# A third bank for the attention scores, and one bank less for the stages around them

## The chip, the cores and the metric

The kernel runs on 1 core of one Trainium2 chip. The metric is the device time of one execution in microseconds. The kernel before took 2009.88 us in the median of 3 runs (2007.78 to 2009.91).

## The reference

The input x has 8 sequences of 1024 tokens with 256 features, all in float32. Three blocks follow one another, each added to x:

```python
x = x + 0.5 * ffn(layernorm(x))      # before attention
x = x + attn(layernorm(x))
x = x + 0.5 * ffn(layernorm(x))      # after attention

def ffn(x):                          # same weights both times
    logits = x @ R.T                                 # 8 experts
    gate = softmax(logits) * (one of the top 2)      # then gate / (sum + 1e-6)
    h = einsum('btd,erd->bter', x, A)                # rank 16 per expert
    return x @ W.T + b + einsum('bter,eor->bto', gate[..., None] * h, B)

def attn(x):
    kv = rmsnorm(x @ W_kv) * g_kv                    # rank 64
    q_c = x @ W_q                                    # rank 128
    k = concat(heads(kv @ W_kdec, 16), rope(heads(x @ W_krope, 32)))
    q = concat(heads(q_c @ W_qdec, 16), rope(heads(q_c @ W_qrope, 32)))
    v = heads(kv @ W_vdec, 16)                       # 16 heads
    scores = q @ k.T / sqrt(48), causal
    return softmax(scores) @ v, heads joined, @ W_o
```

## The kernel before, in words

**Tiling.** A sequence is cut in two halves of 512 tokens. The feed-forward parts and the projections work on one half at a time: a "job" (16 jobs before attention, 16 after). Attention works on "quads": 4 heads of one sequence, 32 quads in all, g = 0 to 31. Lane 0 runs 30 jobs one after the other. Lane 1 runs two alone, job 1 at the start and the last one, job 31; its tiles are carved out of `probs`, so in the trace its tiles read `probs`.

**A job on PE.** Each step of a job fills one PSUM bank, which ACT or DVE then empties: tr0, tr1 (transposes of the normed rows, two token tiles each, L692), low0, low1 (low-rank part and gate logits, L699), gated_tr (L704), y0, y1 (main product, L712 and L714); before attention also tr20, tr21 (L692), qc (L721), kv (L727) and kvt (L733); after attention wo0 and wo1 come first (L681). `wj_b` has 2 banks for lane 0, and the steps take them in turn: step number `use` waits until step `use - 2` has been emptied (L666 to L672). Lane 1 takes `o_b` and the second bank of `st_b` in turn. ACT empties most steps (L951); DVE empties wo (L1038) and y (L1132) by adding them to `xa`.

**A quad on PE.** "mx" steps multiply q by k without a mask (48 a quad, L787, 2 banks `mx_b`); DVE takes the row maximum of each (L977, L980). The maxima are folded, transposed ("mx_turn", L793) and sent through a scratch tensor in HBM into the row `SHIFT` of the q tile, so that the score matmul subtracts them. "score" steps compute the transposed scores: 12 strips of 4 heads, each step two matmuls, L755 and L757, into one bank of `st_b`. ACT takes the exponential of each into `probs` (L859), GpSimd zeroes the masked corner (L1169), and "pv" steps (6 a quad, L775) multiply by v into `o_b`. DVE divides (L1002 to L1015), SyncE writes the result to `ao_scratch`, and the job after attention reads it back.

`st_b` has 2 banks. Score number i writes bank `a % 2`, a being the head, and waits for exponential i - 2 (L750). Score matmuls and mx matmuls use float32r; the others use float32. "piece" and "v" steps (L821 to L834) make k, q and v from the projections in the one bank `tp_b`; ACT, GpSimd and DVE apply rope and split each into a high and a low part, and SyncE sends them through HBM scratch into the tiles of the quads.

**The order.** There is no scheduler at run time. A table `ORDER` has one string for each engine, and each letter takes the next step of one stream: on PE, S is a score, X an mx step, V a pv, P a piece, table or v, F an mx_turn, J a step of lane 0 and j one of lane 1. Each engine walks its string in order (`walk`); semaphores alone hold the engines together. Each string is 3892 steps on PE, 2107 on ACT, 2741 on DVE, 543 on GpSimd and 528 on SyncE.

PSUM has 8 banks here: st_b 2, mx_b 2, o_b 1, tp_b 1, wj_b 2.

Of the kernel before, what the change touches and what calls it, by code (L numbers as in the profile page):

```python
# [130 lines left out]
def uses(*steps):  # L131

    out = []
    for n, (m, pair, side) in enumerate(UNIT):
# [1109 lines left out]
```

## Time and profile before

| what | value |
|---|---|
| median of 3 runs | 2009.88 us |
| profiled execution | 2005.28 us |
| its span | 2002.8 us |
| PE busy | 1901.2 us, 95% |
| DVE busy | 1439.5 us, 72% |
| ACT busy | 1024.3 us, 51% |
| GpSimd busy | 849.4 us, 42% |
| mean granted TensorE clock | 0.98 |

All durations come from the profiled execution; the span is that of its instructions, and the execution took 2.5 us more. PE is the matmul row of TensorE and PEld its weight loads, which overlap it. Idle before a row is the idle time of that engine just before it, and the arrow names what ended it. One float32 matmul stands as two rows in the trace and as one in the order.

### The profile page before, as it was taken

Reading aid. Unit: us, or ns where it says so; the run is one execution under the profiler, and the core shown is the slowest. Engines: PE = TensorE matmul, PEld = TensorE weight load, DVE = VectorE, ACT = ScalarE, POOL = GpSimd, SP = SyncE. Lnnn points to the kernel's source line nnn. Section 1 sums busy time; section 2 is a strip of 40 time slices with the busy share of each in tenths; the row PEclk is TensorE's granted clock in tenths of the full one; section 3 lists DMA queues with packets and bytes.
Section 4 is the critical chain, followed back from the end, with each engine's and each line's share of the span. In section 5 each row is a group of like instructions: output and inputs, shape, how many; then the busy total and the mean of one; then the engine's idle time right before and its main releaser. Section 6 shows DMA issues by size and latency. Waiting matters only on the chain.

```text
span 2002.8 us, 32215 instructions
## 1 busy us (share of the span) xinstructions
PE 1901.2 (95%) x10832; PEld 1325.5 (66%) x10832; DVE 1439.5 (72%) x4555; ACT 1024.3 (51%) x2125; POOL 849.4 (42%) x912
## 2 busy tenths in 40 slices
PE   6789999999999999999999999999999999999995
PEld 5446766666677666766677667666767667677554
DVE  5767777777776877778777777788777687677632
ACT  3436554555454554545555545555556455454450
POOL 3446453553433635255441644435453454422121
PEclk9979999999999999999999999999999999999997
DMA  3687666676665666676566576646677566665511
GB/s 101 191 207 173 169 153 173 163 173 152 174 157 123 175 159 162 164 168 162 152 155 162 145 196 161 167 115 171 168 166 196 129 172 160 159 155 122 116 33 45
DMA packets 169812, 307.58 MB, mean 154 GB/s; under 512 B 15088, under 2 KB 33776, under 8 KB 169648
## 3 DMA queue, kind: packets, MB, share of 16 engines
q1 hardware_dynamic: 169648, 305.53, 61.0%
q8 instruction: 86, 1.41, 0.3%
q14 instruction: 78, 0.64, 0.1%
HBM read 179.12 MB, written 126.35 MB: 153 GB/s over the span
## 4 chain that ended last, share of the span: by engine, by line
PE 68%; DMA 10%; DVE 8%; POOL 7%; ACT 2%; issue 2%; SPq 1%; POOLq 0%; DVEq 0%; ACTq 0%
PE st_b L755 12%; PE o_b L775 11%; PE mx_b L787 11%; PE st_b L757 10%; PE tp_b L824 4%; PE wj_b L712 4%; DMA st<-k_scratch 3%; PE tp_b L821 3%; PE wj_b L681 2%; PE wj_b L714 2%; DMA q_scratch<-lo_t 2%; PE wj_b L699 2%; DVE xn L1077 2%; PE wj_b L692 2%; DVE mx_b L977 1%
## 5 line engine op out<-in xcount | busy, mean ns | idle before, releaser
L859 ACT ACTIVATE probs<-st_b 128x512 f32<-128x512 f32 (+3 forms) x1536 | 708.3, 489 | 537.9 <-PE st_b L757 504.4
L977 DVE CUSTOM_DVE_ANT_0 mx_b<-mx_b,tri 128x256 f32<-128x256 f32 (+3 forms) x1024 | 511.0, 515 | 141.2 <-PE mx_b L787 136.9
L755 PE MATMUL st_b<-st 97*128 97x512 f32 (+2 forms) x1536 | 588.2, 387 | 10.6 <-ACT probs L859 6.8
L787 PE MATMUL mx_b<-st 96*128 96x256 f32 (+2 forms) x1536 | 565.5, 411 | 12.4 <-DVE mx_s L980 6.3
L757 PE MATMUL st_b<-st,k_st 96*128 96x512 f32 (+2 forms) x1536 | 533.4, 351 | 0.0
L1169 POOL TENSOR_SCALAR_AFFINE_SELECT probs<-probs 128x512 f32<-128x512 f32 x256 | 168.2, 660 | 607.9 <-ACT probs L859 607.5
L980 DVE TENSOR_REDUCE mx_s<-mx_b 128x1 f32<-128x512 f32 (+1 forms) x512 | 333.2, 651 | 117.0 <-PE mx_b L787 110.4
L787 PEld LDWEIGHTS mx_b<-st 96*128 96x128 f32 x1536 | 282.0, 191 | 169.6 <-issue 80.1
L755 PEld LDWEIGHTS st_b<-st 97*128 97x128 f32 x1536 | 293.1, 191 | 134.7 <-issue 61.4
L757 PEld LDWEIGHTS st_b<-st,k_st 96*128 96x128 f32 x1536 | 294.9, 192 | 33.0 <-issue 9.8
L775 PE MATMUL o_b<-probs,v_s 128*17 128x512 f32 (+3 forms) x3072 | 285.7, 490 | 2.0 <-POOL probs L1169 1.9
L775 PEld LDWEIGHTS o_b<-probs,v_s 128*17 128x17 f32 x3072 | 70.9, 97 | 142.8 <-issue 111.7
L977 DVE DVE_READ_ACCUMULATOR2_ANT mx_s<- 128x1 f32 x1024 | 143.2, 140 | 0.0
L523 POOL TENSOR_TENSOR rot<-rot,cos_t 128x512 f32<-128x512 f32 x62 | 79.1, 1276 | 148.6 <-ACT rot L872 148.5
L872 ACT ACTIVATE rot<-tp_b 128x512 f32<-128x512 f32 x124 | 74.0, 597 | 107.1 <-PE tp_b L824 65.5
L712 PE MATMUL wj_b<-w_s,xt 128*128 128x256 f32 x480 | 123.9, 380 | 1.3 <-ACT xn L951 1.3
L907 ACT ACTIVATE hi_t<-rot 128x1024 fp32r<-128x1024 f32 x62 | 65.6, 1058 | 104.3 <-POOL rot L529 104.1
L824 PE MATMUL tp_b<-stg,wkr_s 128*128 128x512 f32 x240 | 114.9, 601 | 1.6 <-ACT rot L872 0.9
L1132 DVE SCALAR_TENSOR_TENSOR xa<-wj_b,xa 128x512 f32<-128x512 f32 x60 | 41.4, 690 | 89.3 <-PE wj_b L714 89.2
L1192 POOL TENSOR_TENSOR xa<-xa,hb_s 128x256 f32<-128x256 f32 x120 | 93.1, 802 | 24.8 <-DVE xn L1077 24.8
L1077 DVE TENSOR_SCALAR xn<-xa,mv,rs 128x256 f32<-128x256 f32 x180 | 95.4, 577 | 7.0 <-POOL rs L1185 5.8
L712 PEld LDWEIGHTS wj_b<-w_s,xt 128*128 128x128 f32 x480 | 88.6, 190 | 13.2 <-ACT xn L951 2.4
(189 smaller groups left out, 2302.7 us busy)
## 6 DMA issues: line engine op xcount, KB each, us to landing
st<-q_scratch SPq DMA_DIRECT2D x128, 384.0 KB, 5.9
st<-k_scratch SPq DMA_DIRECT2D x128, 384.0 KB, 8.7
k_st<-k_scratch SPq DMA_DIRECT2D x128, 384.0 KB, 10.4
q_scratch<-hi_t SPq DMA_DIRECT2D x32, 768.0 KB, 3.8
q_scratch<-lo_t SPq DMA_DIRECT2D x32, 768.0 KB, 5.2
k_scratch<-hi_t SPq DMA_DIRECT2D x30, 768.0 KB, 4.3
k_scratch<-lo_t SPq DMA_DIRECT2D x30, 768.0 KB, 4.6
ao_scratch<-o_f SPq DMA_DIRECT2D x256, 32.0 KB, 1.8
```

The lines of the kernel that those rows point to most:

```text
L712: nc.tensor.matmul(dst, xt[:, tk, P * kk:P * kk + P], w1_s[:, kk, 0:D], start=(kk == 0), stop=False)
L755: nc.tensor.matmul(dst, k1_st[u][0:SHIFT + 1, a, P * j:P * j + P], q_st[u][0:SHIFT + 1, a, q0:q0 + w], start=True, stop=False)
L757: nc.tensor.matmul(dst, k2_st[0:SHIFT, a, P * j:P * j + P], q_st[u][0:SHIFT, a, q0:q0 + w], start=False, stop=True).then_inc(st_full, 1)
L775: last = nc.tensor.matmul(o_b[32 * a:32 * a + DV + 1, 0, q0 - HALF * h2:q0 - HALF * h2 + n], v_s[g // NQ % 2][:, j, HQ * q + a, :], probs[ ...
L787: nc.tensor.matmul(mx_b[:, m % 2, 0:w], q_st[u][0:SHIFT, a, P * i:P * i + P], k1_st[u][0:SHIFT, a, k0:k0 + w], start=True, stop=True).then ...
L824: last = nc.tensor.matmul(dst, wkr_s[:, kk, k, eight], own.stg[:, :, P * kk:P * kk + P], start=(kk == 0), stop=(kk == KD - 1))
L859: nc.scalar.activation(probs[:, a, PLACE[s]:PLACE[s] + n], st_b[:, a % 2, HALF - n:HALF], ACT.Exp, scale=SCALE).then_inc(exp_done, 1)
L977: nc.vector.tensor_tensor_reduce(src, src, tri[:, HALF - n:HALF], 1.0, NEG, ALU.add, ALU.max, dst).then_inc(mx_done, 1)
L980: nc.vector.tensor_reduce(dst, src, AX_X, ALU.max).then_inc(mx_done, 1)
L1077: last = nc.vector.tensor_scalar(own.xn[:, tk, :], own.xa[:, tk, :], own.mv[:, tk, 0:1], own.rs[:, tk:tk + 1], ALU.subtract, ALU.mult)
L1169: nc.gpsimd.affine_select(out=d, in_=d, compare_op=ALU.is_ge, fill=0.0, base=0, pattern=[[0, HQ], [1, P]], channel_multiplier=-1).then_inc ...
L1192: last = nc.gpsimd.tensor_tensor(own.xa[:, k, :], own.xa[:, k, :], hb_s[:, :], ALU.add)
```

## The change

`st_b` gets 3 banks and `wj_b` keeps 1. Score i takes bank `i % 3` and waits for exponential i - 3. Each lane has one bank (`wj_b` for lane 0, `o_b` for lane 1), so every step of a job waits until the step before it has been emptied. Lane 1 no longer uses `st_b`, so the first scores no longer wait for job 1. All five strings of `ORDER` are replaced; they hold the same number of each letter as before.

```diff
@@ ORDER, one line of 38 of the PE string @@
-        "SXSXSXVXXPSXSXPXSXSPXXSSXXXXXFXXPXXVSSXPXXSSPXXSSXSXSXJFXXSSXVXXSSXJXXSSXPXSXSPXXSSPXXSSVXXSSJXSXSPXXSSV"
+        "SSXPXSXSSPXXSSSVXXXXXXPXXVPXXFXXPXXXXJXXJXXSSXSXSJXXSSSXXFSSXSXSXSSXSXSSXSXSSSXXVXXPSXXSSPXSXSSXSPXXSSSVX"
...
-        st_b = bank("st_b", 2)
+        st_b = bank("st_b", 3)
         mx_b = bank("mx_b", 2)
         o_b = bank("o_b")
         tp_b = bank("tp_b")
-        wj_b = bank("wj_b", 2)
-        lanes = [Lane(sb, [wj_b[:, 0, :], wj_b[:, 1, :]], sb("stg", [P, GT, STGW]), sb("kvs", [P, GT, P]), ""),
-                 Lane(carve, [o_b[:, 0, :], st_b[:, 1, :]], probs[:, :, late:late + STGW],
+        wj_b = bank("wj_b")
+        lanes = [Lane(sb, [wj_b[:, 0, :]], sb("stg", [P, GT, STGW]), sb("kvs", [P, GT, P]), ""),
+                 Lane(carve, [o_b[:, 0, :]], probs[:, :, late:late + STGW],
...
-            return lanes[LANE[n]].banks[bank_use(n, name) % 2]
+            return lanes[LANE[n]].banks[0]
...
-                if name == "wo0" and use:
+                if use:
                     pe.wait_ge(own.wj_free, use)
-                elif use > 1:
-                    pe.wait_ge(own.wj_free, use - 1)
...
                         pe.wait_ge(row_set, g + 1)
-                        pe.wait_ge(lanes[1].wj_free, len(job_mm(1)))
-                    if i > 1:
-                        pe.wait_ge(exp_done, i - 1)
+                    if i > 2:
+                        pe.wait_ge(exp_done, i - 2)
                     w = max(n, WIDE)
-                    dst = st_b[:, a % 2, HALF - w:HALF]
+                    dst = st_b[:, i % 3, HALF - w:HALF]
...
-                    nc.scalar.activation(probs[:, a, PLACE[s]:PLACE[s] + n], st_b[:, a % 2, HALF - n:HALF], ACT.Exp,
+                    nc.scalar.activation(probs[:, a, PLACE[s]:PLACE[s] + n], st_b[:, (UNITS * g + HQ * s + a) % 3, HALF - n:HALF], ACT.Exp,
```

Three places of the order follow. The line numbers of the changed kernel are smaller: L749 and L751 are the score (before L755 and L757), L781 is mx, L690 a transpose, L697 low, L702 gated_tr, L708 and L710 y, L679 wo, L769 pv.

PE, a middle quad, around the steps low0 and low1 of a job, before:

```order
L787 MATMUL mx_b<-st 128x512
L699 MATMUL wj_b<-w_s,xt 128x136 x4
L787 MATMUL mx_b<-st 128x512
L755 MATMUL st_b<-st 128x384
L757 MATMUL st_b<-st,k_st 128x384
L787 MATMUL mx_b<-st 128x512
L755 MATMUL st_b<-st 128x384
L757 MATMUL st_b<-st,k_st 128x384
L699 MATMUL wj_b<-w_s,xt 128x136 x4
```

and the corresponding place after:

```order
L749 MATMUL st_b<-st 128x256
L751 MATMUL st_b<-st,k_st 128x256
L749 MATMUL st_b<-st 128x256
L751 MATMUL st_b<-st,k_st 128x256
L781 MATMUL mx_b<-st 128x384
L697 MATMUL wj_b<-w_s,xt 128x136 x4
L781 MATMUL mx_b<-st 128x512
L781 MATMUL mx_b<-st 128x384
L697 MATMUL wj_b<-w_s,xt 128x136 x4
```

Before, a score stood alone between mx steps and several steps lay between low0 and low1; after, scores come in pairs or threes, and two mx steps lie between low0 and low1.

PE, the end of the last quad, before (the last gated_tr, a score, y0 and y1, pv, then wo0 and wo1 of lane 1 in two banks):

```order
L704 MATMUL wj_b<-ident,xn 128x128 x4
L755 MATMUL st_b<-st 128x256
L757 MATMUL st_b<-st,k_st 128x256
L712 MATMUL wj_b<-w_s,xt 128x256 x2
L714 MATMUL wj_b<-bt_s,xn 128x256
...
L775 MATMUL o_b<-probs,v_s 17x256 x4
L775 MATMUL o_b<-probs,v_s 17x128 x4
L681 MATMUL o_b<-wo_s,probs 128x256 x4
L681 MATMUL st_b<-wo_s,probs 128x256 x4
```

and after:

```order
L749 MATMUL st_b<-st 128x256
L751 MATMUL st_b<-st,k_st 128x256
L769 MATMUL o_b<-probs,v_s 17x256 x4
L769 MATMUL o_b<-probs,v_s 17x128 x4
L702 MATMUL wj_b<-ident,xn 128x128 x4
L708 MATMUL wj_b<-w_s,xt 128x256 x2
L710 MATMUL wj_b<-bt_s,xn 128x256
...
L679 MATMUL o_b<-wo_s,probs 128x256 x8
```

The last pv has moved ahead of gated_tr, y0 and y1 of lane 0, and lane 1's wo0 and wo1 share one bank.

SyncE, the head, around the first shift (L643 sends it, L647 reloads it as a row, L613 stores a unit of q or k, L624 loads a half of a quad), before:

```order
L624 DMA st<-q_scratch 48x4x512 x2
L624 DMA st<-k_scratch 48x4x512 x2
L643 DMA shift_scratch<-shift 16x128
L624 DMA st<-q_scratch 48x4x512 x2
L624 DMA st<-k_scratch 48x4x512 x2
L647 DMA st<-shift_scratch 1x4x512
L613 DMA q_scratch<-hi_t 384x1x512
L613 DMA q_scratch<-lo_t 384x1x512
```

and after:

```order
L613 DMA q_scratch<-hi_t 384x1x512
L643 DMA shift_scratch<-shift 16x128
L613 DMA q_scratch<-lo_t 384x1x512
L647 DMA st<-shift_scratch 1x4x512
L624 DMA st<-q_scratch 48x4x512 x2
L624 DMA st<-k_scratch 48x4x512 x2
```

The four loads between shift and row have moved behind the row, and the two stores have moved ahead of them.

## Rows read from the trace of the kernel before

**Rows 1.** The page, busy time of each engine and share of the span.

```profile
PE 1901.2 (95%) x10832; PEld 1325.5 (66%) x10832; DVE 1439.5 (72%) x4555; ACT 1024.3 (51%) x2125; POOL 849.4 (42%) x912
```

**Rows 2.** Timeline of a middle quad: start us, us, engine, line, operation, tiles, shapes.

```profile
1023.00 0.40 PE L755 MATMUL st_b<-st 97*128 97x512 f32 x1
1023.23 0.40 PE L757 MATMUL st_b<-st,k_st 96*128 96x512 f32 x1
```

**Rows 3.** Windows: us, busy of PE, PEld, DVE, ACT, POOL, clock, DMA, GB/s.

```profile
0.00:50.00 50.00, 33.84 (x164) 27.83 (x165) 29.59 (x120) 19.30 (x32) 19.41 (x32) 0.93 0.33 102
...
1000.00:1100.00 100.00, 99.59 (x584) 72.02 (x581) 74.54 (x243) 53.76 (x111) 32.47 (x37) 1.00 0.66 158
...
1950.00:2003.00 53.00, 27.22 (x119) 22.08 (x118) 12.13 (x45) 4.46 (x12) 6.62 (x10) 0.77 0.13 42
```

**Rows 4.** Waits of the weight loads, whole span: us in total, times, longest.

```profile
PEld st_b L755 <- issue: 61.4, 138, 1.9
PEld st_b L755 <- ACT probs L859: 45.7, 146, 1.1
...
PEld mx_b L787 <- DVE mx_s L977: 30.9, 98, 2.3
PEld mx_b L787 <- DVE mx_s L980: 26.9, 65, 2.5
...
PEld wj_b L712 <- ACT xn L951: 2.4, 3, 1.0
```

**Rows 5.** Timeline of the last quads: one score kept back.

```profile
1907.11 0.28 PE L755 MATMUL st_b<-st 97*128 97x256 f32 x1
...
1907.23 0.28 PE L757 MATMUL st_b<-st,k_st 96*128 96x256 f32 x1
...
1907.75 0.19 PEld L755 LDWEIGHTS st_b<-st 97*128 97x128 f32 x1 [0.44 <-ACT probs L859]
1907.75 0.39 PE L755 MATMUL st_b<-st 97*128 97x256 f32 x1 [0.23 <-ACT probs L859]
...
1907.97 0.28 PE L757 MATMUL st_b<-st,k_st 96*128 96x256 f32 x1
```

**Rows 6.** Groups by shape, ACT and DVE: busy us, mean ns, idle before.

```profile
L859 ACT ACTIVATE probs<-st_b 128x512 f32<-128x512 f32 x768 | 436.5, 595 | 273.7 <-PE st_b L757 253.1 <-PE o_b L775 8.6
...
L1132 DVE SCALAR_TENSOR_TENSOR xa<-wj_b,xa 128x512 f32<-128x512 f32 x60 | 41.4, 690 | 89.3 <-PE wj_b L714 89.2
```

**Rows 7.** Timeline of the head: a bank filled, emptied, and the next matmul.

```profile
26.93 0.60 PE L704 MATMUL wj_b<-ident,xn 128*128 128x128 f32 x4
...
27.57 0.60 ACT L951 ACTIVATE xn<-wj_b 128x512 f32<-128x512 f32 x1
...
28.31 1.10 PE L712 MATMUL wj_b<-w_s,xt 128*128 128x256 f32 x4 [0.78 <-ACT xn L951]
```

**Rows 8.** Timeline of the end.

```profile
1952.21 1.10 PE L712 MATMUL wj_b<-w_s,xt 128*128 128x256 f32 x4 [0.54 <-ACT xn L951]
1952.30 0.63 POOL L1169 TENSOR_SCALAR_AFFINE_SELECT probs<-probs 128x512 f32<-128x512 f32 x1 [1.40 <-ACT probs L859]
...
1957.56 0.84 PE L775 MATMUL o_b<-probs,v_s 128*17 128x256 f32 x16
...
1967.98 3.64 PE L681 MATMUL o_b<-wo_s,probs 128*128 128x256 f32 x8 [9.58 <-DMA probs<-ao_scratch]
...
1980.70 2.18 PE L699 MATMUL o_b<-w_s,probs 128*128 128x136 f32 x8
```

**Rows 9.** Waits of the weight loads from 1900 us on.

```profile
PEld st_b L755 <- ACT probs L859: 9.3, 26, 0.7
```

**Rows 10.** Timeline of the head: weights landed, the shift row, the first score.

```profile
15.41 0.69 DVE L1069 COPY lo_t<-sin_s 128x1024 f32<-128x1024 f32 x1 [3.10 <-DMA sin_s<-in_sin]
...
113.74 0.73 SPq L647 DMA_DIRECT2D st<-shift_scratch  x1
...
121.00 0.80 PE L755 MATMUL st_b<-st 97*128 97x512 f32 x1 [0.47 <-DMA st<-shift_scratch]
```

More of the change, by code:

```diff
@@ new lines @@
+        "XSSSJXSXSXSXSVXXSSSXSXSSPXXSSSPXXSSSFXXJPXXJVXXJPXXSSXSXSSXSXJXSSSXSXSXFVXXPXSXSXSXSXPXXVPXXSSSXSXPXJXVX"
+        "XJXXSSSJXXSSSPXXSSSPXXSSSPXXSSSSXJXVFXXJSXXSSXSXJXXSSSJXXSVXXVSXXSSSJXSSXSSXSXSSXSFXSSXSXSVXXPXSXSSSXPXV"
+        "JXXSPXXSSSXXVXXPXXSSSXVXXSSSXPXXSSSPXXSSSVXXSSSXSXFSXSXSXSXSPXXSSSVXXSSSPXXSSSSXXSSSXSXSSPSSSFVPSSXXSPXX"
+        "SVXXJPXXSSSXSXJXXVXXPXXSSPXXSSSXSXSJXXSSSVXXSSSXVXXSSSXXSSSXVXXSSSXSSXSFXSSVXXJSXSXJXXSSJXXSSSXSXSSXSXSS"
+        "SXSXSSXXFVXSXSXSSJXXVXXJSVXXJXXSSJXXSSSPXXSSSPXXSJSXSSXJXXSSJXXSSSXSPXSXSSVXXSSSPSSSJSXPJXXVFJXXPJXXVXXS"
@@ new lines @@
+        "SSXSXSSXPXSSSXSSXJXSSJXXSSJFXXVXXPXSSXXSSPXXVXXPSXXSSPXXSSSVXXSJSXSSXJXSSXSJXXSSXJXSSXSSXSSXPXXSSSPXXVFX"
+        "XJPXXSSJXXSSSVXXSJXXSSSXSXSSXSXSSSXVXFXVSXSXSSJXSXSJXSXSJXXVXXJXXSSSXPXSXSXSPXJXSPXXJXXSSSJXXSSSPXXSSSXV"
+        "XXPXSXSSJSXXFSJXSXPJXXSSVJXXSSSXPXSSSPXSSXSSXSXSPXVPJSSSJFSVJXXPSXSXSXSPXXVXPXXSSSXSXPXVXXVXXSSXSXSXSSSS"
+        "XSSXSVXXSSJSXSXJXSSXXJSXSXJXSXSSVFXXSSSXSXSSVXXSSSSXXSSXSXSSXXJSXSXJXXSSJFXXSSSXVXXSSXSXSVXXVXXJSSSXJXSS"
+        "XJXXSSSJXXSSSPXXSSSXSXSJXSXSJXXSSJXXSSSPXXSVXPXSXSSXVFXXSSVXXPXXSSSPJXXSSJXXSSJXXSJXXSSSXSXPSXSXSVXXSFSS"
@@ new lines @@
+        "XPJXSXPJXXPJXXPVXXPSXXSSSXSXSSPXXSSSVXXSSSPXXSSJSXSXJXSSXJXSXJXSXFSXSVXXPXSXSSVXXSSSSSXSXSSXSXJSXSXJXXSS"
+        "JFXXSVXXVSXXSSSXXSSSVXXJSSXJXSXSJXXSSJXXSPXSXSSPXXSSJXPXJXXSSSJXXSSPXXVVXXSSSXPSJSXFXSSJXXPJXXSSSJXXSSSX"
+        "SSXSPXSSXPXSXSPVXPJSSFSJPSJPVXXPXXSSXSXSXPXXVXXSVXXSSXSXVXXSSSXSXSSXSXSSXSVXXSSSJXXJXXJXSXJXSXSXSSVFXXSS"
+        "SXSXSSXSXSVXXSSSXSXSSXSXJXSSXJXXSSJFXXSSSXSXSSXSXVXXSVXXSSJXSXSJXSXSJXXSSJXXSSSPXXSSSPXXJSSXSJXXSSJXXPVX"
+        "XVXSXSSPSJSXSSXJFXSXSSJXXSSSJXXSSXSXSSSXSPXXVPJXXSSJXXSSJFXXVVXXSSSXXSSSXXSPXXSVXXPXSXSSXSPXSXSPXXSSSPSX"
@@ L183 @@
+        "JSSSVSSSSSSSJSSSJVJSSSJSSSVSSSSVJJJjjjjjjjjj",
         "",
@@ L208 @@
+        "EEEJEEEEEJEEEEEEEEEEEEEEEEEEEEEEEEEEEEEEEEEEEEEEEEEEEEEEEEEEEEEEEEEEEEEEEEEEEEEEEEEEEEEEEEEEEEEEEEEEEEEE"
+        "EEJEEJEJEEEJEEEJEEEEJjjjjjj",
         "",
@@ L237 @@
[L237 to L238 removed]
+        "JwJJJJjjjwwjjJJJJJJJJJJjjjjjjjjjjJJJJJjJJjjjjjjJJJLJJjLRLJLJjLRLLLMMJMMJJMMJJJMMJJJMMJMMMMMLJMfJJLMMJMMn"
+        "JMMJMMJMMMMMMLMMMMLMMMMMMMMMMMLMMLMMfooooMMnMMMMMMLMMMMMMLMMfJMMnMJMMJMMJMMJMMJMMJMMMMMMMLMMMMMLMMMMMMMf"
+        "MMnMMMMLoMMooMMoMMMLMMJMfMJMnJJJMMJMJMJMJMMJMMoooMMoMMMMLMMJMMLJMMJJJMMJMMJMMLMMfnMMMMMMLMMMMJMMJMMoMMoJ"
@@ L239 @@
+        "fJJMnMooMMoMMoMMLMJMJJJMJMJMJMJMJfJLnJJLoMMooMMoMMLMMMMMMMMMMLMMMLMMJMMMMMMJMMJJMMJMMfoMnMJJMMooMMoMMooM"
+        "MooMMJMMJMMfJMnMJMJMMJJJJJMMMMMMJMMJMMMMMMMMMMMJMMJMMJMMJMMfJMnMoMMJJMMooMMoMMoMoMoMMJoMMfJMMnJMJMMJJMMJ"
+        "JJJMMMMMMJMMJMMMMMMMMMMMMMoMMoooMMfMMnMoMMoMMoMMoMMMMMMfMnMMMMMMMMMMMMMMMMMMMMMMMMMMoMMoooMMoMofonoJJJJJ"
+        "JJJJJJJJJJJJooooJJjjjjjjjjjjjjjjjjjjj",
         "",
@@ L705, in job @@
                 elif name in ("y0", "y1"):
-                    if k == 0:
-                        pe.wait_ge(own.wj_free, bank_use(n, "gated_tr") + 1)
                     for tt in range(2):
@@ L717, in job @@
                         pe.wait_ge(w2_in, 16 * N_W2)
-                    pe.wait_ge(own.wj_free, bank_use(n, "tr21") + 1)
                     nx = own.stg
```

170 lines of the change are left out of this document (73 added, 97 removed).

## The prediction

> **What bounds the kernel now.** I read the page's busy times first, then the table of stretches, who the weight loads waited for, and last single stretches of the timeline. The page shows PE busy for 95% of the span and DVE for 72% [rows 1]. By that alone 101 us (2002.8 less 1901.2) could be saved. But a matmul's row is drawn longer than the time it holds the next one up: 512 columns start 0.23 us apart and are drawn 0.40 long [rows 2], 256 columns start 0.12 apart and are drawn 0.28 long [rows 5]. A stall of a tenth or two hides under such a row, so I look at the weight loads, which start only when their wait is over. The Trainium skill says this too (Perfetto Trace Analysis, Identifying the Most-Contended Engine): a matmul row's busy share is a poor measure of how far PE is from its limit, and the weight loads tell more. The trace agrees: what the loads waited for scores [rows 4] is nearly half of all that is drawn as idle on PE, the end and the head included.
>
> The stretches [rows 3] show three stages: a head, where PE idles 16 of the first 50 us; a middle with PE nearly always drawn busy (one stretch of 100 us stands); an end, where it idles 26 of the last 53. Of the loads' waits [rows 4], 45.7 us in 146 waits are first scores' loads (L755) kept back by the exponential that empties the bank, and 57.8 us in 163 waits are mx loads (L787) kept back by DVE. The stages around attention, which have two banks, wait 2.4 us in all at the y steps (L712), the longest of their lines.
>
> **A third bank for the scores.** Score i now waits for exponential i-3 instead of i-2. What one wait costs is to be seen at 1907.2 [rows 5]: the second matmul of the score before starts at 1907.23, the next score should start at 1907.35, starts at 1907.75, and its own second matmul follows after 0.22 instead of 0.12, since its weight load was no longer hidden: 0.50 lost where the load shows 0.44 idle. Where the matmul before has 512 columns, part of the idle shown is PE still streaming (0.23 us of pitch, 0.19 of load), and the least a wait costs is the exposed load, 0.10. So the 146 waits cost between 15 us (146 by 0.10) and 73 us (146 by 0.50). The mean shown is 0.31 us, mixed in widths; I take three quarters of what is shown, 34 us, since half the scores have 512 columns.
>
> How much of it goes? An exponential takes 0.60 us for 512 columns [rows 6]; with its semaphores some 0.8 us must lie between the end of the score that held the bank and the next one in it. I walked both PE tables step by step with the pitches above (a score two matmuls, an mx step one, the others by their start-to-start times). The tables hold the same steps, so the PE work is the same. Before, 193 of 1534 scores have less than 0.8 us of PE work as cover, 49 of them among the last 90; after, 45 of 1533, 4 of them among the last 90. The count fits the 146 waits seen. What is left is 45/193, so 77% of 34 us goes: **-26 us** (bounds -12 and -56 by the two prices). What hides the exponential now is work that PE does anyway. What is late next is mx, which keeps its two banks: less than 0.8 us of cover stood at 44 mx steps after against 39 before, and the missing time grows by 5.5 us. With 57.8 us shown now, I take **+3 us** (bounds -5 and +15).
>
> **One bank for the stages around attention.** Each of some 315 steps of lane 0 now waits until the step before is evacuated. Three rows of the head price this at its best [rows 7]: the transposes end near 27.5, ACT copies 27.57 to 28.17, the next matmul starts at 28.31, 0.8 us after the end. An addition on DVE takes 0.69 [rows 6]. If ACT is in the middle of an exponential the turn is up to 0.6 longer, 1.4. Before, two such steps had 2.4 us or more between them in the median; after, the median cover is 1.1 to 1.3 us. Of 240 steps in the middle quads, 6 have less than 0.8 (2 us missing in all), 105 have less than 1.3 (26 us missing), 143 less than 1.5 (52 us missing). Queued behind a waiting stage step are the next scores and mx steps, so ACT and DVE run dry too. The value: ACT is busy 51% of the span [rows 1], so about half the steps meet it idle, and cover falls short only for the other half, by part of an exponential: **+5 us**, bounds +2 and +52.
>
> **The end.** Before, the two y steps of the last lane-0 job (5.35 us of PE) stand ahead of the last pv step: the mask is done at 1952.93 and pv starts at 1957.56 [rows 8]. After, pv comes first and gated_tr, y0 and y1 follow it, under the 9.6 us in which PE waits for the round trip through ao_scratch: **-4.6 us**. Against it, the last job in lane 1 has one bank. wo1 waits for the addition to wo0: +0.83 (0.69 and 0.14). Second transposes and their copy come ahead of low0: low0 started at 1980.70 while tr1 ran, and will start 1.95 us later (0.6 copy, 0.14, 0.6 for tr1 at the low clock, and its copy). low1 behind low0's copy: +0.8. y1 behind y0's addition: +0.83. Sum +4.4. wo0 ran its 8 matmuls in 3.64 us, straight after 9.6 us without work, in a stretch with a mean granted clock of 0.77 [rows 3, 8]. With work in the gap it may start at 2.4 instead of 1.2 GHz: 0 to -1.8. I take **-1 us** for the end (bounds -5 and +5). The denser waits of the last 100 us (9.3 us in 26 waits [rows 9]) are in the 34 us above.
>
> **The head.** ACT now does its five weight copies, which wait for the weights that land at 15.4 [rows 10], before the copies of low0 and low1; that and one bank put some 3 us on the first two jobs. Against it, SyncE issues the reload of the shift row ahead of four loads of 384 KB: before, the row left at 113.74 behind them and the first score started at 121.00, 7.3 us later. It also puts one store of 768 KB ahead of the shift itself, which waits for rope. The two cancel as far as I can tell: **0**, bounds -6 and +6.
>
> **Sum.** -26 + 3 + 5 - 1 + 0 = -19. The profiled execution took 2005.28 us, so it becomes 1986; the median of the runs shown stands 4.6 above it, and the forecast for the median is **1991 us**.
>
> **Rivals.**
> 1. *The single bank decides, slower.* Place: the 240 stage steps of the middle. Price: if ACT and DVE come to them behind two queued items, the missing cover counts to 1.5 us: +52 in place of +5, with the rest unchanged +28: 2038; at the 1.4 us of one full exponential about +39, so 2025. It decides once a step loses 0.11 us more on average (26/240). For it: their cover was cut from 2.4 to 1.2. Against it: ACT idles half the time, and only 6 steps miss the bare 0.8. The Trainium skill (Perfetto Trace Analysis, Matmuls) wants independent groups to rotate through banks so that an evacuation overlaps the next group; by that rule the stages lose what the scores gain. Here the groups between two stage steps are scores in other banks, so the rule speaks less against it than it seems.
> 2. *The wait only changes its name.* PE is in order: freed of the exponential it comes to mx sooner, and DVE (72% busy) holds it there. For it: the mx waits are already larger than the scores'. Against it: mx cover hardly changes. The 26 us shrink to a few: 2006 to 2011.
> 3. *More than the waits.* Waits that the views put down to "issue" at L755 (61.4 us, not all pacing) were the bank's too, and the head gains its 6 us: another 20 us off: 1970.
> That the change does not do what it says can be excluded for the bank, not for its worth: that is rival 2.
>
> **Chances.** Forecast 0.60 (its own range 1979 to 2002), rival 1 0.15, rival 2 0.13, rival 3 0.12. Range for 8 in 10: 1969 to 2014. What a measurement can tell here from no change is 0.2%, 4 us. Faster: 0.60 + 0.12 + 0.04 of rival 2 = 0.76; the same 0.07; slower 0.17.
>
> **What would show it.** Right: the scores' load waits put down to the exponential fall from 45.7 to about 10 us; those of wj_b put down to ACT stay under 15; the gap between the last mask and the last pv closes; PE's middle stretches rise toward 99%. Wrong: wj_b loads waiting tens of us (rival 1); mx loads waiting 80 us or more (rival 2); the first score later than 125 us (the head).

## The result, and the profile after

| kernel | median, us | runs | ratio to before, 95% interval |
|---|---|---|---|
| before | 2008.8 (2003.1 to 2009.9) | 4 | |
| changed | 2043.9 (2040.1 to 2047.8) | 4 | 1.018 [1.0151, 1.021] |

The change made the kernel 1.8% slower. The forecast was 1991, faster, with a range to 2014: wrong in sign. The profiled execution took 2041.6 us, its span is 2039.9, so 37 more than before. The page of the changed kernel, its busy times [rows 1]:

```profile
PE 1903.9 (93%) x10832; PEld 1334.8 (65%) x10832; DVE 1424.5 (70%) x4555; ACT 998.7 (49%) x2125; POOL 851.6 (42%) x912
```

PE has the same instructions and nearly the same busy time; 34 us more of its span are drawn idle (136.0 and 101.6). Three stretches (us, busy of PE, PEld, DVE, ACT, POOL, clock, DMA, GB/s) answer to [rows 3]:

```profile
0.00:50.00 50.00, 29.51 (x141) 22.47 (x141) 26.23 (x113) 16.78 (x27) 17.66 (x30) 1.00 0.31 102
1000.00:1100.00 100.00, 92.88 (x537) 63.01 (x536) 68.77 (x219) 44.77 (x98) 47.49 (x50) 0.97 0.61 151
1990.00:2040.00 50.00, 27.14 (x112) 19.99 (x112) 12.26 (x46) 3.69 (x8) 6.76 (x9) 0.75 0.14 45
```

The end looks as before. The head has 141 matmuls in its first 50 us, where it had 164, and has caught up to 3 us at 222 us of PE work. The loss is in the middle: the stretch shown was drawn 99.59 busy and is at 92.88. It is an extreme one; over the 17 stretches from 200 to 1900 us the mean went from 97.9 to 96.4, which is 26 of the 34 us. The waits of the weight loads over the whole span (us in total, times, longest) answer to [rows 4]:

```profile
PEld mx_b L781 <- DVE mx_s L971: 61.9, 140, 1.6
...
PEld mx_b L781 <- DVE mx_s L974: 32.2, 58, 3.1
PEld st_b L749 <- issue: 25.9, 35, 4.9
PEld st_b L749 <- DMA st<-shift_scratch: 20.8, 12, 5.2
...
PEld st_b L749 <- ACT probs L853: 14.1, 45, 1.2
PEld mx_b L781 <- DMA st<-k_scratch: 12.3, 7, 3.6
...
PEld wj_b L708 <- ACT xn L945: 2.9, 5, 0.9
```

The reader is to see that the third bank did to its own wait what it was to do: 45.7 us in 146 waits became 14.1 in 45. The stages with one bank hardly wait (all loads of wj_b for ACT and DVE: 5.3 us before, 17.8 now). But loads that wait for DVE's maxima went from 57.8 to 94.1 us, and two kinds of wait are new: for a DMA that brings the row of maxima (shift_scratch; 1.0 us in 1 wait before), and waits of up to 4.9 us under "issue", for which the profile shows no releaser. In the window from 1937 us on, 0.2 us in 1 wait is left of what stood in [rows 9].

Where are the 4.9 us? The timeline of quad 16 shows it, first PE and the queue of SyncE (columns as in [rows 2]):

```profile
1060.28 1.23 SPq L635 DMA_DIRECT2D k_st<-k_scratch x2
...
1069.34 0.66 PE L781 MATMUL mx_b<-st 96*128 96x512 f32 x2
1074.59 0.77 PE L749 MATMUL st_b<-st 97*128 97x512 f32 x1 [4.59 <-issue]
1075.15 0.63 PE L751 MATMUL st_b<-st,k_st 96*128 96x512 f32 x1
1075.58 0.63 PE L749 MATMUL st_b<-st 97*128 97x512 f32 x1
```

and then the landing of these two DMAs of L635 (time from issue), and four stretches around the gap, as above:

```profile
DMA to landing us min/median/max: 11.8/12.8/13.7
```

```profile
1068.00:1072.00 4.00, 1.92 (x12) 1.25 (x10) 3.37 (x7) 1.68 (x3) 4.00 (x5) 1.00 1.07 221
1072.00:1076.00 4.00, 1.42 (x3) 1.16 (x4) 0.17 (x1) 0.18 (x1) 2.52 (x4) 0.64 1.06 161
1076.00:1080.00 4.00, 4.00 (x12) 3.28 (x10) 2.28 (x16) 2.33 (x5) 0.11 (x1) 0.51 1.07 194
1080.00:1084.00 4.00, 4.00 (x38) 2.10 (x40) 2.44 (x10) 1.96 (x6) 0.71 (x2) 1.00 1.05 354
```

`k_st` is the second copy of k, which the second matmul of each score reads; it is one buffer, so the first half of the copy for quad g may be loaded only when the exponentials of the first 8 strips of quad g-1 are done. The second of the two DMAs left at 1060.8 and landed 13.7 later, at 1074.5, and the first score of quad 16 started at 1074.59. After the gap two matmuls of 512 columns start 0.43 us apart (1075.15, 1075.58) instead of 0.23: the granted clock of 1072 to 1080 is 0.64 and 0.51, the lower level, 1.2 GHz. PE had just been idle 4.6 us. So the wait is paid again, in part, as half speed. The Trainium skill describes this (TensorE: Matmul & The Clock Gate, HAM oscillation — how this bites in real kernels): a wait for a DMA lets the clock fall, and the work behind it starts slow. The trace agrees.

The kernel before did the same load with less hurry. Its two DMAs of quad 16, the first score, and the landing:

```profile
1043.03 0.86 SPq L635 DMA_DIRECT2D k_st<-k_scratch x2
...
1055.63 0.47 PE L755 MATMUL st_b<-st 97*128 97x512 f32 x1
```

```profile
DMA to landing us min/median/max: 10.4/11.1/11.7
```

The later one landed at 1055.2, and the first score started 0.4 us behind it. So that trap was already in the trace that I had.

The other new wait, quad 8, second half. L635 is the copy's second half, L787 turns the maxima, L643 sends them, L647 reloads them as a row:

```profile
583.88 0.97 SPq L635 DMA_DIRECT2D k_st<-k_scratch x2
...
589.97 0.30 PE L787 MATMUL tp_b<-ident,mxf 128*72 128x128 f32 x1
...
590.62 0.31 SPq L643 DMA_DIRECT2D shift_scratch<-shift  x1
...
596.44 0.62 SPq L647 DMA_DIRECT2D st<-shift_scratch  x1
598.48 0.19 PEld L749 LDWEIGHTS st_b<-st 97*128 97x128 f32 x1 [4.07 <-DMA st<-shift_scratch]
```

8 KB needed 5.8 us, behind the k copy (2 by 384 KB), which landed at 596.2; SyncE waits for it before it issues the row. The row landed at 598.5, when the first score started. In the kernel before, the first score of a second half started 16.0 us after the row was issued (median of 31 quads, 3.3 to 22.6); in the changed one 2.9 (2.0 to 11.5).

Head and end of the changed kernel, for [rows 8, 10]:

```profile
118.00 0.73 SPq L647 DMA_DIRECT2D st<-shift_scratch  x1
...
125.21 0.40 PE L749 MATMUL st_b<-st 97*128 97x512 f32 x1
...
1990.35 0.63 POOL L1163 TENSOR_SCALAR_AFFINE_SELECT probs<-probs 128x512 f32<-128x512 f32 x1 [2.08 <-ACT probs L853]
1991.03 0.84 PE L769 MATMUL o_b<-probs,v_s 128*17 128x256 f32 x16 [1.07 <-POOL probs L1163]
...
2001.22 1.97 PE L679 MATMUL o_b<-wo_s,probs 128*128 128x256 f32 x8 [1.19 <-DMA probs<-ao_scratch]
```

The last pv follows its mask at once, and wo0 runs in 1.97 us, not 3.64. From the end of the last mask to the end of the span it was 49.9 us, now 48.9.

**Where PE lost time.** A label of idle time says who came last, not what the step cost. So for each PE step I took its start-to-start time less the 15th percentile of such steps (same kind, same kinds around it, nine profiled runs), and booked the rest on the step behind it. In us:

| ahead of | before | changed | after_no_trip | after_no_trip_no_k2 | plan_k_behind_row |
|---|---|---|---|---|---|
| scores | 38.8 | 57.8 | 35.9 | 14.1 | 20.1 |
| mx | 45.2 | 73.0 | 64.9 | 55.8 | 52.5 |
| stage steps | 25.6 | 18.4 | 22.9 | 18.5 | 24.6 |
| pieces, turns, pv | 40.2 | 37.6 | 36.5 | 37.0 | 36.1 |
| sum | 149.8 | 186.8 | 160.2 | 125.4 | 133.3 |

The sums differ by 37.0 between changed and before, as the spans do. (The last three columns are experiments below.) How the loss divides between the rows depends, from one order to another, on which steps are taken as alike. With six other groupings (by the shapes of the step and of its neighbours, and by other percentiles) the loss ahead of mx still rises from before to changed, by 31 to 74 us. But the one ahead of scores moves by anything from -21 to +15, and the one ahead of stage steps rises in five of the six. Between changed, after_no_trip and after_no_trip_no_k2, which have one order, the groupings agree within 5 us. So the table tells what these two experiments took away; from before to changed it tells only that mx lost.

### The profile page after: what moved, and what is told of

The parts are those of the page before. It is cut to its first block, busy times and chain, and to the rows that moved or that the text cites. A ratio compares the mean times of both kernels' runs of the same rounds, so it can differ in the third digit from the quotient of the medians.

```text
span 2039.9 us, 32169 instructions
## 1 busy us (share of the span) xinstructions
PE 1903.9 (93%) x10832; PEld 1334.8 (65%) x10832; DVE 1424.5 (70%) x4555; ACT 998.7 (49%) x2125; POOL 851.6 (42%) x912
## 4 chain that ended last, share of the span: by engine, by line
PE 76%; DMA 9%; DVE 8%; issue 3%; SPq 2%; ACT 1%; POOL 0%; POOLq 0%; DVEq 0%; ACTq 0%
PE mx_b L781 13%; PE st_b L749 12%; PE st_b L751 12%; PE o_b L769 11%; PE tp_b L818 5%; PE wj_b L708 4%; PE tp_b L815 3%; PE wj_b L679 3%; PE wj_b L697 2%; PE wj_b L710 2%; PE wj_b L690 2%; DMA st<-k_scratch 2%; DVE mx_b L971 2%; DMA shift_scratch<-shift 1%; PE wj_b L716 1%
## 5 line engine op out<-in xcount | busy, mean ns | idle before, releaser
L853 ACT ACTIVATE probs<-st_b 128x512 f32<-128x512 f32 (+3 forms) x1536 | 677.9, 492 | 516.4 <-PE st_b L751 330.8
L781 PE MATMUL mx_b<-st 96*128 96x256 f32 (+2 forms) x1536 | 565.5, 417 | 29.9 <-DVE mx_s L974 11.0
L749 PE MATMUL st_b<-st 97*128 97x512 f32 (+2 forms) x1536 | 553.2, 367 | 37.5 <-DMA st<-shift_scratch 17.8
L751 PE MATMUL st_b<-st,k_st 96*128 96x512 f32 (+2 forms) x1536 | 531.1, 353 | 0.0
L781 PEld LDWEIGHTS mx_b<-st 96*128 96x128 f32 x1536 | 278.9, 193 | 223.8 <-issue 93.7
L749 PEld LDWEIGHTS st_b<-st 97*128 97x128 f32 x1536 | 295.3, 192 | 94.1 <-issue 25.9
L751 PEld LDWEIGHTS st_b<-st,k_st 96*128 96x128 f32 x1536 | 297.1, 193 | 30.9 <-issue 4.6
L769 PE MATMUL o_b<-probs,v_s 128*17 128x512 f32 (+3 forms) x3072 | 287.8, 494 | 1.8 <-POOL probs L1163 1.1
L769 PEld LDWEIGHTS o_b<-probs,v_s 128*17 128x17 f32 x3072 | 71.6, 97 | 147.0 <-issue 119.2
L1177 POOL TENSOR_SCALAR ve<-mv 128x4 f32<-128x4 f32 x45 | 15.0, 333 | 308.8 <-DVE mv L1049 308.7
L708 PE MATMUL wj_b<-w_s,xt 128*128 128x256 f32 x480 | 127.0, 388 | 4.3 <-DVE xa L1126 2.5
L708 PEld LDWEIGHTS wj_b<-w_s,xt 128*128 128x128 f32 x480 | 91.3, 193 | 22.9 <-DVE xa L1126 4.2
L1186 POOL TENSOR_TENSOR xa<-xa,hb_s 128x256 f32<-128x256 f32 x120 | 89.6, 774 | 25.7 <-DVE xn L1071 25.7
L815 PE MATMUL tp_b<-stg,wq_s 128*128 128x512 f32 x180 | 93.0, 597 | 1.1 <-issue 0.7
```

Source lines behind the costliest of these rows:

```text
L708: nc.tensor.matmul(dst, xt[:, tk, P * kk:P * kk + P], w1_s[:, kk, 0:D], start=(kk == 0), stop=False)
L749: nc.tensor.matmul(dst, k1_st[u][0:SHIFT + 1, a, P * j:P * j + P], q_st[u][0:SHIFT + 1, a, q0:q0 + w], start=True, stop=False)
L751: nc.tensor.matmul(dst, k2_st[0:SHIFT, a, P * j:P * j + P], q_st[u][0:SHIFT, a, q0:q0 + w], start=False, stop=True).then_inc(st_full, 1)
L769: last = nc.tensor.matmul(o_b[32 * a:32 * a + DV + 1, 0, q0 - HALF * h2:q0 - HALF * h2 + n], v_s[g // NQ % 2][:, j, HQ * q + a, :], probs[ ...
L781: nc.tensor.matmul(mx_b[:, m % 2, 0:w], q_st[u][0:SHIFT, a, P * i:P * i + P], k1_st[u][0:SHIFT, a, k0:k0 + w], start=True, stop=True).then ...
L815: last = nc.tensor.matmul(dst, wq_s[:, k, eight], own.stg[:, :, 2 * P:3 * P], start=True, stop=True)
```

## The experiments

A ratio is to the kernel before, run on the same chip at the same time; 0.1% is 2 us. "Trip" is the round trip of the maxima through HBM.

**1. after_no_trip, before_no_trip.** The trip left out from the third quad on:

```diff
+                elif name in ("shift", "shift_row") and n > 1:
+                    continue
-                        pe.wait_ge(shift_in[u][h2], 16 * (g // 2 + 1))
+                        pe.wait_ge(shift_in[u][h2], 16)
-                        dve.wait_ge(shift_out, 16 * n)
+                        dve.wait_ge(shift_out, 16 * min(n, 4))
```

> The changed kernel without the round trip of the maxima from the third quad on: SyncE no longer sends the 64 rows of maxima to the HBM scratch nor reloads them as a row (two DMAs a half, 60 halves left out), and the scores use the row of quad 0 or 1, so the output is not the reference's. Theory A (the new order of steps puts the first score of a half so close behind its own maxima that PE, which is in order, waits for the trip through HBM): the kernel after measures 2043, and it falls by 25 to 45 us, to 2000 to 2018; the waits put down to shift_scratch (20.8 us of weight loads, 17.8 us of matmuls) are gone and nothing takes their place. Rival B (PE is held by DVE's maxima and the single bank of the stages, and a wait for the trip is only the place where it shows): it falls by less than 10 us, and the mx loads' wait for DVE (94 us) rises by what the trip gave free. Rival C (the lower granted clock of the run after): under 5 us.

> The kernel before with the same left out. Theory A: its first scores wait only 1.0 us of loads for the row, so it falls by 2 to 10 us, to about 2000 to 2006; and the two kernels without the trip stand within 6 us of each other or the changed one ahead by up to 20, which is what the third bank brings. Rival B: the two still stand 25 to 35 us apart.

Measured: 2016.9, ratio 1.0049 [1.0026, 1.0072], and 2000.6, 0.9968 [0.9952, 0.9983]. From 1.018 that is 1.3% (26 us) and 0.3% (6 us). Theory A had the size, but its second half failed: the two stay 0.8% (16 us) apart instead of within 6 us. So there was a second cause.

**2. old_order_new_banks, new_order_old_banks, old_order_one_bank.** Tables and banks crossed. The third is the first with the scores held to two banks:

```diff
-        st_b = bank("st_b", 3)
+        st_b = bank("st_b", 2)
-                    if i > 2:
-                        pe.wait_ge(exp_done, i - 2)
-                    dst = st_b[:, i % 3, HALF - w:HALF]
+                    if i > 1:
+                        pe.wait_ge(exp_done, i - 1)
+                    dst = st_b[:, i % 2, HALF - w:HALF]
```

> The changed kernel's banks (3 for scores, 1 for the stages) under the order of the kernel before. With one bank the old order would stand still at some steps, so a step was moved ahead there and nowhere else: 61 of 3892 positions on PE differ from the old order. Theory A: the single bank costs some here, since the old order puts less between two stage steps (low0 and low1, y0 and y1), and the third bank gives 20 to 30 back: 1990 to 2020, faster than the changed kernel by 20 us or more; first scores wait under 5 us for shift_scratch. Rival B (the single bank is what costs): 2040 or more, with tens of us on wj_b loads.

> The banks of the kernel before (2 and 2) under the new order, again with steps moved ahead only where it would stand still: 277 positions on PE differ, since the new order puts scores in threes and two banks do not carry that. Theory A: slower than the changed kernel, 2060 to 2200: the threes of scores meet an exponential each (0.3 to 0.5 us at some 500 scores) and the trip is as late as in the changed kernel. If it comes out below 2043, the new order is not what costs and the banks are.

> As old_order_new_banks (the order of the kernel before, repaired for one bank of the stages), but the scores keep their two banks, so one PSUM bank lies unused. It parts that run's +37 us: the single bank of the stages by itself, and the third bank by itself. Expected: the third bank is worth what the losses ahead of scores show (39 us before, 23 with three banks) and what was 45.7 us of load waits on the exponential and became 19.4, so 15 to 28 us: this run at 2058 to 2071, and the single bank alone costs 52 to 65 us under the old order. If it measures 2043 to 2048, the third bank is worth nothing.

Measured: 2043.0, 1.0169 [1.0142, 1.0196]; 2197.1, 1.0929 [1.0896, 1.0963]; 2050.5, 1.022 [1.0192, 1.0247]. The expectation of the first failed: under the old order the new banks are as slow as the changed kernel, for another reason. One bank for the stages alone costs 2.2%, 44 us (loss ahead of stage steps 25.6 to 52.8 by the measure above; 13 us of it in the first 170 us), and the third bank then gives back 0.5%, 10 us, which with these intervals is 2 to 18; the spans say 7 (2051.1 and 2044.0). The third run was expected at 2058 to 2071 and lies below. The loads' waits on the exponential and those of wj_b, of old_order_one_bank:

```profile
PEld st_b L754 <- ACT probs L858: 44.4, 143, 1.0
...
  ACT xt L950: 11.2, 18
  ACT hl L950: 10.2, 13
  DVE xa L1131: 8.7, 8
```

and of old_order_new_banks:

```profile
PEld st_b L754 <- ACT probs L858: 19.4, 83, 0.4
```

25.0 us less are drawn as wait, and 7 to 10 us less are measured. The second run falls in its range, but moves 277 PE positions, too many to price one part by it: it shows only that the new order, with its threes of scores, leans on three banks (loads waited 305.0 us in 561 waits for the exponential).

**3. after_short_max, before_short_max.** DVE reads 128 columns of each mx block:

```diff
-                    src = mx_b[:, m % 2, 0:n]
+                    src = mx_b[:, m % 2, n - P:n]
```

> The changed kernel with DVE reading only the last 128 columns of each mx block (the maximum over the rest is left out, so the output is not the reference's). Nothing else changes: same steps, same waits, same DMAs. DVE's 1536 maxima take some 0.25 us in place of a mean 0.64. Theory D (beside the trip, what the changed kernel lost is DVE's pace: measured by start-to-start times over what a step streams, PE loses 75 us ahead of mx steps from 200 to 1900 us, against 16 in the kernel before): it falls by 50 to 90 us, to 1950 to 1990, the loads of mx wait under 10 us for DVE, and the trip's waits shrink too since the maxima are done sooner. Rival E (the mx waits are slack that would show elsewhere, at the exponential or the single bank): it falls by under 20 us more than the kernel before does.

> The kernel before with the same left out. Theory D: it has 27 us ahead of its mx steps, so it falls by 15 to 35 us, to 1970 to 1990; its waits for the exponential (45.7 us) grow or stay. The changed kernel with short maxima is then level or up to 25 us ahead, which is the third bank's worth when DVE holds nobody. Rival E: the two stay 25 us or more apart, the changed one behind.

Measured: 2027.5, 1.011 [1.0085, 1.0134], and 1977.6, 0.9875 [0.9848, 0.9902]. The changed kernel falls by 0.7% (14 us), the kernel before by 1.3% (25 us). Theory D is refuted, rival E stands: DVE's pace is not what sets the changed kernel back. In after_short_max:

```profile
PEld st_b L749 <- DMA st<-shift_scratch: 23.6, 12, 4.9
PEld mx_b L781 <- DVE mx_s L971: 22.4, 55, 1.8
...
PEld mx_b L781 <- DVE mx_s L974: 14.7, 17, 2.9
```

94.1 us of waits on DVE became 37.1, and 14 us came of it. The waits for the row did not shrink with them (20.8 to 23.6).

**4. after_no_k2, after_no_trip_no_k2, before_no_trip_no_k2.** The k copy is loaded once, for quad 0:

```diff
+                elif name == "k2" and n:
+                    continue
-                        pe.wait_ge(k2_in[h2], 32 * (g + 1))
+                        pe.wait_ge(k2_in[h2], 32)
...
```

The edit has one place more: SyncE's stores of q and k no longer wait for the copy either. And since SyncE no longer issues it, it no longer stands still for the exponentials that free the copy's buffer, so that the loads behind it in SyncE's string can leave sooner. The runs with the trip left out have the edit of experiment 1 too.

> The changed kernel without the round trip of the maxima (as in the run before) and also without reloading the second copy of k (k_st, one buffer): it is loaded for quad 0 alone, and all scores use that, so 124 DMAs of 196 KB are left out and the output is not the reference's. In the changed kernel the first score of quads 12, 13, 16, 17 and 20 starts 0.1 us after that copy has landed. Theory G (two loads, each free of the other, came too close behind their use: the row of the maxima and the copy of k): a further 12 to 25 us less than without the trip (2017), to 1990 to 2005. If the wait falls to something else (rival E): within 6 us of 2017.

> The kernel before with the same left out. It waits 4 us ahead of first scores once the trip is gone, so 2 to 8 us under 2001: 1993 to 1999. By theory G it is then level with the changed kernel (within 8 us), since nothing of the loads' distance is left between them.

> The changed kernel without reloading the k copy (quad 0's is used by all), the trip kept. With the trip left out too it fell by 59 us, with the trip alone left out by 27. If the two add, 2043 less 32: 2008 to 2015. If the k copy is also what makes the trip late (theory H), it falls by more than 32, to 1990 to 2005, and the wait on shift_scratch is under 6 us.

(By the profile such a DMA moves 384 KB, not the 196 or 192 that the expectations name.) Measured: without both 1984.5, 0.9905 [0.9881, 0.9929], against 1988.9, 0.9918 [0.9891, 0.9944] for the kernel before: level. Without the k copy alone 1990.4, 0.9927 [0.9906, 0.9949]. The first two fell 5.5 and 4 us below their ranges (1990 to 2005, 1993 to 1999), the third is in its range, though 9.1 us of waits for the row are left where under 6 were expected. So the k copy alone is 2.5% (51 us), both are 2.75% (55), and the trip is worth 1.3% with the copy there and 0.2% without: they do not add, and most of what the trip costs is the copy's doing. What the loads of mx and scores waited for, in after_no_trip_no_k2, with mx as it was:

```profile
PEld mx_b L785 <- DVE mx_s L975: 60.6, 141, 1.8
...
PEld mx_b L785 <- DVE mx_s L978: 32.1, 58, 3.1
...
PEld st_b L753 <- ACT probs L857: 15.1, 49, 1.3
PEld mx_b L785 <- DMA st<-k_scratch: 12.1, 7, 3.9
...
PEld st_b L753 <- issue: 7.5, 28, 0.8
```

The long waits under "issue" (25.9 in 35, longest 4.9) are gone, so they were waits for the k copy. The kernel before gains 0.8% by the same edit, so that much of the 55 us is not this change's: the part that the change brought is 2.75 less 0.8, 1.9%, which is all of it. This does not part the waits, the traffic on the DMA engines and SyncE's standing still.

Level does not mean that the banks did nothing. In before_no_trip_no_k2 the loads of scores wait for the exponential and those of mx for DVE:

```profile
PEld st_b L759 <- ACT probs L863: 46.7, 147, 1.0
PEld mx_b L791 <- DVE mx_s L981: 32.7, 106, 1.7
...
PEld mx_b L791 <- DVE mx_s L984: 25.0, 66, 1.5
```

Against it the changed kernel waits 31.6 us less for the exponential (15.1) and 35.0 us more for DVE (92.7 against 57.7), at the same time.

**5. after_k_behind_row, after_both_ahead.** Nothing left out, SyncE's string alone changed. First, in 31 quads, the second half of the k copy goes behind the row; then, in 25 quads, its first half also goes ahead of the next quad's loads:

```diff
 L643 DMA shift_scratch<-shift 16x128
-L635 DMA k_st<-k_scratch 48x4x512 x2
 L647 DMA st<-shift_scratch 1x4x512
+L635 DMA k_st<-k_scratch 48x4x512 x2
```

> The changed kernel with one thing changed on SyncE and nothing on the other engines: in 31 quads the load of the second half of the k copy stands behind the row of maxima's reload instead of ahead of it. Everything is computed. Theory H (the trip is late because its two DMAs of 8 KB are queued behind and among the k copy's 2 by 192 KB): it falls by 12 to 28 us, to 2015 to 2031, and the loads' wait on shift_scratch from 20.8 us to under 6. If it is distance on PE alone (maxima too late for the first score, whatever the queue), within 5 us of 2043. Rival: the k copy now comes too late for the ninth strip of scores, and it measures 2043 or more.

> after_k_behind_row, and in 25 quads the load of the first half of the k copy also stands ahead of the four loads of the next quad's half (384 KB each) instead of behind them, again on SyncE alone. If its place on SyncE is what delays first scores: the 17 us ahead of first scores of a first half fall below 6 and the kernel by a further 10 to 25 us, to 2014 to 2029. If the loads it now passes become late in turn (the mx loads' wait on k_scratch, 19.7 us, grows by what is won): within 6 us of 2039, or above.

Measured: 2038.7, 1.015 [1.013, 1.0171], and 2032.0, 1.0141 [1.0101, 1.0181]. From 1.018 that is 0.3% and 0.4%, with intervals that overlap, and both fall short of what was expected (2015 to 2031, 2014 to 2029). In after_k_behind_row the 8 KB of quad 8 and its whole-span waits:

```profile
DMA to landing us min/median/max: 2.5/2.5/2.5
```

```profile
PEld mx_b L786 <- DMA st<-k_scratch: 19.7, 7, 5.3
...
PEld st_b L754 <- DMA st<-shift_scratch: 10.1, 10, 4.9
```

The trip is as short as said (5.8 to 2.5 us) and its waits halve (20.8 to 10.1), but mx now waits 19.7 us for its k, where it was 12.3. With both edits the loss ahead of first scores of a first half falls from 16.8 to 1.6 us as said, and a part of it turns up elsewhere (mx 76.1 to 79.3, stage steps 22.7 to 26.6). Pushing one load forward pushes another back.

**6. new_plan_3_1, new_plan_2_2, head_then_plan_3_1, plan_k_behind_row, plan_both_ahead.** Orders of my own, to see whether the division of banks or the order decides, and to beat both.

> The banks of the changed kernel (3 for scores, 1 for the stages) under a third order: derived from the order of the kernel before by letting each engine's next step pass over one that would still have to wait, with 1.1 us and more allowed to each DMA. If the order is what costs (theory A with D: trip and maxima too close), this one has neither: waits for shift_scratch under 3 us, loss ahead of mx and stage steps together under 60 us: 1930 to 1985. If three and one banks are the wrong division whatever the order (rival F), it measures 2000 or more, with the wait on wj_b's loads the largest.

> The banks of the kernel before (2 and 2) under an order derived in the same way. It tells what the third bank is worth when either division has an order of its own. If the third bank is worth what I predicted (some 20 us), 1955 to 2000 and 10 to 30 us behind the plan with three banks; if the division does not matter, within 8 us of it.

> A try at a version that beats both, with the changed kernel's banks. The derived order with 3 and 1 banks (new_plan_3_1, 2019) lost 21 us in the first 170 us against the kernel before and gained 8 from there on. This one has the changed kernel's order for the first 172 us (3 us behind before) and the derived order from there on: 1995 to 2006, level with the kernel before or a little ahead.

> The same move on SyncE in head_then_plan_3_1 (2001), in 29 quads. Its first scores lose under 4 us, so there is little to gain: 1996 to 2006; slower if the k copy then comes too late for its own scores.

> The same in plan_k_behind_row (1995), in 30 quads. Its first scores of a first half lose 2.5 us, so there is nothing to win there, and the loads passed come later: 1994 to 2006.

| run | median, us | ratio, 95% interval |
|---|---|---|
| new_plan_3_1 | 2018.9 | 1.0069 [1.0045, 1.0093] |
| new_plan_2_2 | 2016.4 | 1.0057 [1.0039, 1.0075] |
| head_then_plan_3_1 | 2000.8 | 0.9974 [0.996, 0.9988] |
| plan_k_behind_row | 1994.6 | 0.9942 [0.9922, 0.9961] |
| plan_both_ahead | 2042.7 | 1.02 [1.0155, 1.0245] |

With orders derived in one way the two divisions are 0.1% apart, inside the intervals. Both missed their ranges; nor was it rival F's wj_b, since in new_plan_3_1 it is mx that loses most (its loads wait 96.9 us for DVE). With the changed kernel's head in front, three and one banks beat the kernel before by 0.26%, and with the row ahead of the k copy by 0.58%, 12 us: the best version here, with nothing left out. The last run is the lesson: one more swap on SyncE in 30 quads, nothing else, and it is 48 us slower by the medians, 2.6% by the ratios, where 1994 to 2006 was expected. The loads of mx that wait on k, in plan_k_behind_row:

```profile
PEld mx_b L786 <- DMA st<-k_scratch: 1.6, 1, 1.6
```

and in plan_both_ahead:

```profile
PEld mx_b L786 <- DMA st<-k_scratch: 33.2, 14, 3.9
```

## Why the prediction was wrong

**Right.** The loads' wait on the exponential fell to 14.1 us (forecast: about 10). Those of wj_b stayed under 15. The gap between the last mask and the last pv closed, and the end gained 1.0 us as forecast (-1). One sign of being right failed: PE's middle stretches fell (97.9 to 96.4 in the mean) instead of rising toward 99%.

**The failed step.** It is the sum itself: it has no term for the DMAs of the middle. Of SyncE's new string I looked only at the head. I walked the PE tables for the cover of each bank, and never set the issue and landing of the row and of the k copy against the first score that needs them. In the kernel before, 1055.2 against 1055.6 could be read. The runs put there what the forecast lacked: without trip and copy the changed kernel is 2.75% faster and the kernel before 0.8%, a difference of 1.9%, against the 1.8% that the change cost. No rival had this mechanism; a wait that is bound by a transfer was missing among them. The trace shows how: SyncE issues the k copy 6.2 us (median of 31 quads) after the last score that frees it has started, before 3.2, and the row's reload stands behind the copy's second half in 31 quads, before in 10. The first score of a quad starts within 1 us of the copy's landing in 12 of 31 quads, before in 5. PE's new order has a share in it that is easily missed: from the weight load that turns the maxima of a second half (L793, now L787) to the first score of that half it was 21.5 us (median of 31 quads), and is 6.8 now, while SyncE sends them 0.8 us behind the turn in both kernels. No run changed this distance alone, and moves on SyncE alone gave back 0.3 to 0.4%, so how the 1.9% divides between PE's order and SyncE's is not shown.

The transfers are not the whole miss. Without them the change is worth -4 us (1984.5 against 1988.9, inside the intervals) where the sum said -19: the other terms together were off by some 15 us, and the next paragraphs say in which.

**The third bank, -26.** Mis-sized. The wait it takes away is real and went (45.7 to 14.1; under the old order 44.4 to 19.4), yet in one order it is worth 7 to 10 us (2 to 18 by the intervals). The price of a wait was taken as if PE would keep what it saves. It reaches the next hold sooner, and that is rival 2 in kind: loads waited 94.1 us for DVE instead of 57.8, more than the 80 that I had named as its sign. Short maxima gave 14 us, so it is not what made the kernel slower. But it is what became of the gain: with the transfers out, 31.6 us less of one wait stand against 35.0 us more of the other, and the time is level.

**mx, +3.** Mis-sized: bounds -5 to +15, and the loss ahead of mx rose by 27.8 us (45.2 to 73.0), by more in the other groupings of steps. 17.2 went with trip and copy (to 55.8). That leaves 10.6 above the kernel before as it is; the same edit takes some 10 us off that kernel's loss ahead of mx too (read with another grouping), so the new order itself costs nearer 20. The term counted PE work between mx steps against 0.8 us and left DVE's queue out.

**One bank for the stages, +5.** Small, as forecast, as far as it can be read: the loads of wj_b wait 12.5 us more for ACT and DVE (5.3 to 17.8), while the table has the loss ahead of stage steps fall by 7 us and five of the six other groupings have it rise, by up to 19. Rival 1 had a true mechanism (44 us under the old order), which the new table had paid for; the cover that I counted said so. What the table gave for it, distance on SyncE and DVE, I did not count.

**The head, 0.** At the same PE work (222 us) the changed kernel stands 3 us behind, inside the bounds; the first score came at 125.21, 0.2 past my sign for a wrong head.

**The clock.** It was in no term of the middle. Summing 1 less the granted clock over stretches of 4 us under 0.98 from 130 to 1880 us gives 11.8 us for the kernel before, 25.7 for the changed one, 13.7 in after_no_k2 and 6.8 with the trip gone too. So up to 14 us of the 37 are half speed behind long waits. That is read off, not tested by itself. Not every wait was followed by it: from 130 to 1880 us PE idles 13 times for 1.5 us or more, and in the 4 us behind 8 of these the clock was at the lower level for a part, behind one of 3.2 us (at 317 us) not at all.

**Open.** How the k copy's 51 us divide into the waits for it, its load on the DMA engines and SyncE's standing still for its buffer was not parted: edits that only moved it gave 0.4%, the one that removed it 2.5%.

## What to carry to other kernels

When a table or a queue is reordered, list every transfer that a hot step waits for, with its issue, its landing and its first user, before and after; a distance of under a microsecond in the old trace is a price that the new order may charge more often (here in 12 quads instead of 5). A freed wait in an in-order engine is worth what the next hold leaves of it: here 25 us of drawn waits were 7 to 10 us of time. A long stall on PE can cost more than its length: behind 8 of the 13 stalls of 1.5 us or more, that of 4.6 us among them, matmuls ran at half speed for a time.

## What the runs showed of the hardware

In quad 8 a DMA of 8 KB took 5.8 us from issue to landing behind two of 384 KB on SyncE's queue, and 2.5 us ahead of them. The Trainium skill says that within one queue of one DMA engine descriptors start in order, though their writes need not end in order (DMA: Bandwidth & Descriptors, Two DMAs through the same engine are not ordered). What the trace shows fits it: the small one landed 0.2 us after the large ones. Whether another engine's queue would let it pass was not tried.

I had not expected the order of one queue to weigh so much: moving one pair of loads past four others in 30 quads made 48 us by the medians, 2.6% by the ratios, with no compute engine's order touched.

Behind a float32 step the next matmul is drawn early: a piece of two float32 matmuls takes 0.86 us, but an mx behind it is drawn 0.46 after its start, and the mx behind that one 0.63 later instead of 0.23. Such gaps are read over three steps, not one.
